# A second level of product sums on GpSimd, eight transposes for sixteen, and routing as a sign, in a gated long-convolution and attention layer

## The reference, cut to what matters

```python
def _L0_xattn_ref(k, v, q, ssm_kernel, D, head_dim):     # k = v = ctx, q = layernorm(x)
    kv = einsum('bhil,bhjl->bijhl', k_, v_)              # products of every two rows of a group
    y = causal convolution of kv with ssm_kernel (by FFT)
    out = y + kv * D
    out = einsum('bijhl,bhil->bjhl', out, q_)            # weighted by q, summed over i (8 terms)

def _L0_ffn_ref(x, conv_w, Wq, Wk, Wv, Wg, router_w, Wout):   # 16 heads, DK 256, DV 512
    x = silu(x_prev * conv_w[:, 0] + x * conv_w[:, 1])
    q, k, v, g = silu(x @ Wq), x @ Wk, x @ Wv, x @ Wg
    q, k = rotary(q), rotary(k)
    logits = einsum('bhld,hdr->bhlr', v, router_w)       # RATIO = 2 routes
    scores = softmax(logits); onehot = one_hot(argmax(scores), 2)
    norm = 1 / running count of onehot
    q_exp = q[..., None, :] * (scores * onehot)[..., None] * norm
    k_exp = k[..., None, :] * onehot[..., None]
    qk = (q_exp @ k_exp^T) * HDK ** -0.5, lower triangle
    o = layernorm over each head of (qk @ v)
    return (silu(g) * o) @ Wout

x = x + tanh(g_xattn) * _L0_xattn_ref(ctx, ctx, layernorm(x), ...)
x = x + tanh(g_ffn) * _L0_ffn_ref(layernorm(x), ...)
```

## Time and profile before

| what | value |
|---|---|
| median of 3 executions | 910.64 us (909.43 to 911.76) |
| the profiled execution | 909.48 us, its span 907.7 us |
| PE busy | 863.7 us, 95% of the span |
| DVE busy | 712.7 us, 79% |
| POOL busy | 725.8 us, 80% |
| ACT busy | 434.6 us, 48% |
| chain that ended last | 88% of it on PE |

### The profile page before, as it was taken

How to read it: one execution, slowest core, us unless ns; L and a number is a source line. 1 busy time by engine, 2 the same in 40 slices (tenths; PEclk the granted TensorE clock), 3 DMA queues, 4 the chain that set the end, 5 groups by cost and what they waited for, 6 DMA issues and landing times.

```text
span 907.7 us, 17997 instructions
## 1 busy us (share of the span) xinstructions
PE 863.7 (95%) x6592; PEld 732.3 (81%) x6592; DVE 712.7 (79%) x1521; ACT 434.6 (48%) x941; POOL 725.8 (80%) x611
## 2 busy tenths in 40 slices
PE   4889999999999999999999999999999999999974
PEld 3768888888888888888888888888888888888762
DVE  4788877787887778788777878877787897778741
ACT  3655455444545544454554544455454545544320
POOL 6779888899888889988888998888899888886331
PEclk9999999999999999999999999999999999999995
DMA  9310222211222221122222112222211222210000
GB/s 268 106 53 1 65 65 65 64 32 36 63 65 65 65 64 35 34 63 66 64 65 65 38 30 63 65 65 65 65 40 28 63 65 65 65 48 12 4 15 18
DMA packets 26679, 51.83 MB, mean 57 GB/s; under 512 B 3232, under 2 KB 4640, under 8 KB 26592
## 3 DMA queue, kind: packets, MB, share of 16 engines
q1 hardware_dynamic: 22320, 46.19, 19.1%
q10 hardware_dynamic: 4272, 4.48, 1.5%
HBM read 42.12 MB, written 8.55 MB: 56 GB/s over the span
## 4 chain that ended last, share of the span: by engine, by line
PE 88%; issue 4%; DVE 3%; POOL 2%; ACT 1%; DMA 1%; POOLq 0%; SPq 0%; ACTq 0%; DVEq 0%
PE bank L335 38%; PE bank L306 24%; PE bank L284 9%; PE bank L293 6%; PE bank L387 4%; PE bank L372 4%; PE bank L319 2%; PE bank L322 1%; DVE z_terms L844 1%; DMA z_terms<-in_L_xattn_D 1%; PE bank L445 0%; POOL kv L695 0%; POOL rstd L710 0%; POOLq L67 0%; POOL o_rstd L710 0%
## 5 line engine op out<-in xcount | busy, mean ns | idle before, releaser
L306 PE MATMUL bank<-kv_pair,toep 128*128 128x512 f32 x960 | 244.9, 401 | 1.3 <-DVE z_terms L835 1.3
L704 POOL TENSOR_TENSOR kv_pair<-kv,kv_pair 128x576 fp32r<-128x576 f32 x126 | 179.0, 1432 | 51.3 <-ACT kv_pair L537 51.3
L306 PEld LDWEIGHTS bank<-kv_pair,toep 128*128 128x128 f32 x960 | 175.0, 189 | 41.7 <-DVE z_terms L835 6.7
L695 POOL TENSOR_TENSOR kv<-kx 128x512 f32<-128x512 f32 x128 | 173.0, 1351 | 5.6 <-DMA kx<-in_ctx 3.9
L710 POOL TENSOR_TENSOR o_rstd<-o_ve,minus_half 128x16 f32<-128x16 f32 x32 | 93.1, 2908 | 83.5 <-DVE o_ve L921 83.5
L537 ACT ACTIVATE kv_pair<-kv 128x576 fp32r<-128x576 f32 x128 | 87.8, 687 | 106.8 <-POOL kv L698 105.9
L335 PE MATMUL bank<-w_all_high,yT_high 128*128 128x512 f32 (+2 forms) x512 | 120.9, 358 | 0.8 <-DVE gated L952 0.8
L844 DVE TENSOR_TENSOR z_terms<-z_terms 128x512 f32<-128x512 f32 (+1 forms) x96 | 116.6, 1240 | 0.0
L335 PE MATMUL bank<-w_all_low,yT_high 128*128 128x512 f32 (+2 forms) x512 | 112.6, 342 | 0.0
L1017 DVE SCALAR_TENSOR_TENSOR out_sb<-bank,gates,x 128x512 f32<-128x512 f32 x32 | 24.0, 751 | 106.0 <-PE bank L335 106.0
L335 PE MATMUL bank<-w_all_high,yT_low 128*128 128x512 f32 (+2 forms) x512 | 105.9, 339 | 0.0
(11 more groups left out here) (110 smaller groups left out, 1595.9 us busy)
## 6 DMA issues: line engine op xcount, KB each, us to landing
toep<-taps_dram SPq DMA_DIRECT2D x31, 512.0 KB, 7.1
kx<-in_ctx SPq DMA_DIRECT2D x32, 384.0 KB, 7.4
x_in<-in_x SPq DMA_DIRECT2D x32, 256.0 KB
out_x<-out_sb SPq DMA_DIRECT2D x32, 256.0 KB
wv_t<-in_L_ffn_Wv ACTq DMA_DIRECT2D x1, 1024.0 KB, 8.0
w_g<-in_L_ffn_Wg ACTq DMA_DIRECT2D x1, 1024.0 KB, 6.9
w_out<-in_L_ffn_Wout ACTq DMA_DIRECT2D x1, 1024.0 KB, 10.5
w_qk<-in_L_ffn_Wq ACTq DMA_DIRECT2D x1, 512.0 KB, 4.5
```

The costliest lines, as they stand in the source:

```text
L306: ins = nc.tensor.matmul(bank[lc % 2][:, :], toep[:, 1 - p, a, (lc - mc) * P:(lc - mc + 1) * P], kv_p[b][:, 1 - p, mc, 0:FULL], start=(mc ...
L695: eng.tensor_tensor(view(kv[:, c % 2, 0:FULL], [[ROW, NROT], [1, ROW]]), view(kx[:, p, c, 0:ROW], [[0, NROT], [1, ROW]]), view(kx[:, p, c, ...
L704: eng.tensor_tensor(kv_p[1][:, p, c, :], kv[:, c % 2, :], kv_p[0][:, p, c, :].bitcast(F32), ALU.subtract).then_inc(kv_ready[c], 1)
```

## The change

- `add_halves` now runs twice in a step: chunks 0 and 1, and chunks 2 and 3 together. A second level of sums, `add_quarters`, runs on POOL, in two instructions in each step (chunks 0 and 1, then 2 and 3; each adds 2 x 256 columns to 2 x 256 columns). They stand in POOL's list after the rotary sum and ahead of products 2 and 3 (in step -1 after them). `add_transposed` transposes two blocks for each chunk, 8 matmuls instead of 16, and waits for `quarter_done` of POOL instead of `sum_done` of DVE.
- PE projects the gate ahead of `add_transposed`.
- The two `sel` comparisons go; `u` is made twice as wide in one instruction. POOL's rotary sum writes straight into `qke`, and its two products with the sine become one. DVE's `signed_copy` writes a second copy of q and k, times +1 or -1, in place of `expand`. Scores of two rows with different signs cancel, those with equal signs count twice, and the mask's scale is halved. `signed_copy` stands ahead of `ratio` and `gatedT_low` in DVE's list, right behind the second `add_halves`.
- DVE multiplies o by the gate first (`o_gated`, before `norm_x`), and by the power later. The projection of v waits for `o_gated`.
- ACT's gate and its round of products 2 and 3 change places with each other and with the copies of `qke`.

```diff
@@ tensor
-                    eng.wait_ge(sum_done[max(c, 1)], h1 + 1)
-                    for i in range(NROT):
+                    eng.wait_ge(quarter_done[c // 2], h1 + 1)
+                    for i in range(NROT // 2):
...
-                        eng.wait_ge(o_normed, h)
+                        eng.wait_ge(o_gated, h)
                     project(bank[4], yT_p, w_all_p, V0, DV, v_ps, y_low, h + 1)
...
+                if back:
+                    if can_wait(h):
+                        eng.wait_ge(mask_done[2], h)
+                    if h == 0:
+                        eng.wait_ge(g_low, 1)
+                    project(bank[5], yT_p, w_all_p, G0, DV, g_ps, y_low, h + 1)
                 if front:
                     if pre and h != -1:
                         eng.wait_ge(qx_ready, h + 3)
                     add_transposed(h + 1)
@@ scalar
+                if back:
+                    eng.wait_ge(g_ps, h + 1)
...
+                    eng.activation(gate_sb[:, :], bank[5][:, :], ACT.Silu).then_inc(gate_ready, 1)
                 if pre and h != -1:
                     kv_round(p, 2, h + 2)
-                    kv_round(p, 3, h + 2)
...
+                if pre and h != -1:
+                    kv_round(p, 3, h + 2)
@@ gpsimd
+            def add_quarters(half, h1):
+                eng.wait_ge(sum_done[2 * half + 1], h1 + 1)
+                n = NROT // 2 * ROW
+                z = z_terms[:, 2 * half:2 * half + 2, :]
+                eng.tensor_tensor(z[:, :, 0:n], z[:, :, 0:n], z[:, :, n:2 * n], ALU.add).then_inc(quarter_done[half], 1)
...
-                    for a in range(2):
-                        s = const[:, C_SIN + a * hf:C_SIN + a * hf + 1]
-                        eng.tensor_tensor(rot_b[:, :, a * hf:(a + 1) * hf], qk_sb[:, :, (1 - a) * hf:(2 - a) * hf],
-                                          view(s, [[0, 2 * RH], [1, hf]]), ALU.mult).then_inc(rot_prod, 1)
-                    eng.wait_ge(rot_prod, 3 * h + 3)
-                    eng.tensor_tensor(rot_a[:, :, :], rot_a[:, :, :], rot_b[:, :, :], ALU.add).then_inc(rot_ready, 1)
+                    sin = const[:, C_SIN:C_SIN + 1]
+                    eng.tensor_tensor(view(rot_b[:, 0, 0:1], [[HDK, 2 * RH], [hf, 2], [1, hf]]),
+                                      view(qk_sb[:, 0, hf:hf + 1], [[HDK, 2 * RH], [-hf, 2], [1, hf]]),
+                                      view(sin, [[0, 2 * RH], [hf, 2], [1, hf]]), ALU.mult).then_inc(rot_prod, 1)
...
+                    eng.tensor_tensor(qke[:, :, :, 0], rot_a[:, :, :], rot_b[:, :, :], ALU.add).then_inc(rot_ready, 1)
+                if front and h != -1:
+                    add_quarters(0, h + 1)
+                    add_quarters(1, h + 1)
                 if pre:
                     products(t, p, 2, h + 2)
                     products(t, p, 3, h + 2)
+                if h == -1:
+                    add_quarters(0, h + 1)
+                    add_quarters(1, h + 1)
@@ vector
-            def expand():
...
+            def signed_copy():
+                eng.scalar_tensor_tensor(out=qke[:, :, :, 1], in0=qke[:, :, :, 0], scalar=2.0,
+                                         in1=view(u[:, 0, 0:1], [[1, 2 * RH], [0, HDK]]), op0=ALU.mult, op1=ALU.mult
+                                         ).then_inc(qke_ready, 1)
...
+                    eng.wait_ge(gate_ready, h)
...
+                    eng.tensor_tensor(gated[:, :], bank[4][:, :], gate_sb[:, :], ALU.mult).then_inc(o_gated, 1)
                 if pre and h != -1:
                     norm_x(t, p, h)
...
-                    d = view(bank[6][:, DK:DK + 1], [[0, 2], [1, RH]])
-                    eng.tensor_scalar(sel[:, :, :, 0], d, 0.0, None, ALU.is_le)
-                    eng.tensor_scalar(sel[:, :, :, 1], d, 0.0, None, ALU.is_gt)
-                    eng.tensor_scalar(u[:, :], bank[6][:, DK:DK + RH], 0.0, 0.5, ALU.is_gt, ALU.subtract).then_inc(u_ready, 1)
+                    eng.tensor_scalar(u[:, :, :], view(bank[6][:, DK:DK + 1], [[0, 2], [1, RH]]), 0.0, 0.5, ALU.is_gt, ALU.subtract).then_inc(u_ready, 1)
...
                     eng.tensor_tensor(gated[:, :].rearrange("p (a n) -> p a n", n=HDV),
-                                      bank[4][:, :].rearrange("p (a n) -> p a n", n=HDV),
-                                      view(o_rstd[:, 0:1], [[1, RH], [0, HDV]]), ALU.mult).then_inc(o_normed, 1)
...
+                                      gated[:, :].rearrange("p (a n) -> p a n", n=HDV),
+                                      view(o_rstd[:, 0:1], [[1, RH], [0, HDV]]), ALU.mult).then_inc(gated_ready, 1)
...
                     multiply(p, 3, h + 1)
-                    add_halves(slice(2, 3), h + 1)
-                    add_halves(slice(3, 4), h + 1)
+                    add_halves(slice(2, 4), h + 1)
...
+                    eng.wait_ge(u_ready, h + 1)
+                    signed_copy()
```

More of the change, by code:

```diff
@@ L116, in flamingo_gated_layer @@
         ad = sb("ad", RH)
-        u = sb("u", RH)
-        sel = sb("sel", 2, RH, RATIO)
+        u = sb("u", 2, RH)
         th = sb("th", RH)
@@ L208, in flamingo_gated_layer @@
         sum_done = [sem(f"sum_done{i}") for i in range(CH)]
+        quarter_done = [sem(f"quarter_done{i}") for i in range(2)]
         (mul_last, y_conv, out_ready, ad_ready, u_ready, th1_ready, rth1_ready, ratio_ready, eps_ready,
          qke_ready, bn1_done, mv1_done, ve1_ready, nmr1_ready, qn_ready, x2_ready, bn2_done, mv2_done,
-         ve2_ready, nmr2_ready, z_ready, o_summed, o_ve_ready, o_normed, gated_ready) = (
+         ve2_ready, nmr2_ready, z_ready, o_summed, o_ve_ready, o_gated, gated_ready) = (
             sem(n) for n in ("mul_last", "y_conv", "out_ready", "ad_ready", "u_ready", "th1_ready", "rth1_ready",
@@ L214, in flamingo_gated_layer @@
                              "nmr1_ready", "qn_ready", "x2_ready", "bn2_done", "mv2_done", "ve2_ready",
-                             "nmr2_ready", "z_ready", "o_summed", "o_ve_ready", "o_normed", "gated_ready"))
+                             "nmr2_ready", "z_ready", "o_summed", "o_ve_ready", "o_gated", "gated_ready"))
         FIRST, LAST = -2, NH
@@ L444, in step @@
                     eng.wait_ge(qk_copied, h + 1)
-                    nc.tensor.matmul(bank[6][:, 0:RH], rank, u[:, :], start=True, stop=True).then_inc(cnt_ps, 1)
+                    nc.tensor.matmul(bank[6][:, 0:RH], rank, u[:, 0, :], start=True, stop=True).then_inc(cnt_ps, 1)
                 if pre and h != -1:
@@ L949, in step @@
                     eng.wait_ge(o_rstd_ready, h)
-                    if can_wait(h - 1):
-                        eng.wait_ge(gatedT_ps, h - 1)
+                    eng.wait_ge(o_gated, h)
                     eng.tensor_tensor(gated[:, :].rearrange("p (a n) -> p a n", n=HDV),
-                                      bank[4][:, :].rearrange("p (a n) -> p a n", n=HDV),
-                                      view(o_rstd[:, 0:1], [[1, RH], [0, HDV]]), ALU.mult).then_inc(o_normed, 1)
-                    eng.wait_ge(o_normed, h)
-                    eng.wait_ge(gate_ready, h)
-                    eng.tensor_tensor(gated[:, :], gated[:, :], gate_sb[:, :], ALU.mult).then_inc(gated_ready, 1)
+                                      gated[:, :].rearrange("p (a n) -> p a n", n=HDV),
+                                      view(o_rstd[:, 0:1], [[1, RH], [0, HDV]]), ALU.mult).then_inc(gated_ready, 1)
                 if back:
@@ L974, in step @@
                                       gatedT_p[0][:, :, :].bitcast(F32), ALU.subtract).then_inc(gatedT_ready, 1)
-                if h == 0:
-                    eng.wait_ge(qk_low, 1)
-                    eng.wait_ge(g_low, 1)
-                if back:
-                    eng.wait_ge(rot_ready, h + 1)
-                    if can_wait(h):
-                        eng.wait_ge(keT_ps, h)
-                        eng.wait_ge(qeT_ps, h)
-                    expand()
                 if setup_step:
@@ L1039, in shape_constants @@
     centre = np.eye(P) - heads @ heads.T / HDV
-    parts = [np.eye(P), same * HDK ** -0.5, rank, cos, cos, -sin, sin, np.eye(P)[:, ::-1], centre, heads]
+    parts = [np.eye(P), same * HDK ** -0.5 / 2, rank, cos, cos, -sin, sin, np.eye(P)[:, ::-1], centre, heads]
     return np.concatenate([a.astype(np.float32) for a in parts], axis=1)
```

39 lines of the change are left out of this document (21 added, 18 removed).

## The result

The changed kernel takes 913.59 us (median of 7 executions, 910.84 to 915.5), the kernel before 910.32 us beside it (7 executions, 908.37 to 911.76). The ratio is 1.0041, with a 95% interval of 1.0024 to 1.0058: slower by 0.4%. That is a small loss, and the two ranges overlap, but the interval leaves out 1. The prediction was 916 us, 897 to 934.

What follows compares the result with a forecast made beforehand. TensorE (PE) was taken to bound each step. Profiled 909.48 us plus 29 full steps x 0.2 minus 1 at the edges gave 914.3; the median 1.16 above made 915.5, rounded to 916 us, range 897 to 934.

Steps and rivals of the forecast that it cites:

- The blocks: DVE instructions with two SBUF inputs and POOL products or sums exclude each other; held ones end 0.56 to 1.20 us later.
- the layout: DVE and POOL rows of a full step laid out by that exclusion; last quarter add ends at 458.06, +0.1 us a step.
- First close call: POOL's cosine, issued 0.03 us after the second product of `multiply_last`, might win; then net +0.3 us a step.
- the two other orders: Cosine ahead of that product, +0.3 us a step, or add of chunks 0 and 1 ahead of the cosine, +0.5.
- the queue: Ten DVE and POOL instructions from 448.6 on pass one at a time; their own times add up to 9.4 us.
- PE's side: In each full step eight fewer transposes save 0.88 us; the last four come 1.0 us late with refill.
- The edges: Steps outside the full ones: +1.5 us in step -1, savings in steps 30 to 32; together -1 us.
- the signs: Expected after the change: POOL quarter adds of 1.6 to 1.8 us, PE idle 0.7 to 1.2, steps of 26.5 to 27.0.
- The cover for z: In a full step z is ready about 0.4 us early, so PE transposes it without a wait.
- POOL's late finish is absorbed: POOL idles 1.63 us before o's power, so its delay isn't handed on to the next step.
- o times gate first: `o_gated` comes 4 us before `o_normed` did; the projection of v gains slack and no time.
- The rival in time: Second quarter add done by 457.0, so PE's saving is kept, down to 884 us; chance 0.23.

Runs made afterwards that it cites:

- e3: The changed kernel with DVE's signed copy moved behind `ratio` and `gatedT_low`; 908.52 us, 0.9984 of the kernel before.
- e7: The changed kernel with DVE multiplying o by the power first and the gate second again; 907.2 us, 0.997 of the kernel before.
- e5: The changed kernel with quarter adds on DVE in two instructions, POOL's products 2 and 3 held for them; 882.25 us, and 881.41 us beside e8.
- e8: The kernel before with only the sums' part of e5, without the sign or the new order of o's products; 889.6 us, ratio 0.9783.
- e6: The changed kernel with one more POOL product of 192 columns between the quarter adds; 932.0 us, 1.0242 of the kernel before.
- e2: The changed kernel with the gate's projection behind the transposes of the sums again; 1040.17 us, 1.1428 of the kernel before.

## Why the prediction was right

- **The blocks** were right. Moved by 6.86 us, the layout gave 456.96, 458.04, 459.19, 459.75 and 460.92 for cosine, first add, sine, product of o and rotary sum; the rows say 456.96, 458.04, 459.21, 459.76 and 460.92. It gave 464.92 for the last quarter add; it ended at 464.98.
- **First close call**: the cosine, issued 0.03 us behind the second product of `multiply_last`, lost (0.41 us for DVE, 1.54 for POOL). So the order of the main layout held, and neither of the two other orders came. The x power, from 454.90 to 455.45, didn't block `multiply_last` either (the product of 455.04 took its 0.42 us inside it), for which the prediction had 924 us. The Trainium skill, page SBUF — State Buffer (Who interferes with whom), has whoever issues first hold the shared pair of ports for the whole instruction, and the other blocked until then. These rows disagree: both ran at once, neither longer than alone (0.55 and 0.42 us).
- **A close call that I missed**: DVE's second add was laid out as issued at 453.98, 0.08 us ahead of POOL's quarter add. It waits 0.1 us for its own products' signal (460.93 to 461.03), so the quarter add went first. The sum of turns is nearly the same, the end moved by 0.06 us.
- **A miscount**: the prediction has ten instructions in the queue, 6 of POOL and 4 of DVE or so, with 9.4 us. Its own layout has five of POOL and four of DVE, 9.11 us; the other 0.35 us is the end of `multiply_last`. The layout and the sum don't use the count.
- **PE's side**: wait and refill 1.02 us against 1.0; net +0.16 us in this step. The main layout alone gave 0.1; the forecast took 0.2 for an order that didn't come. Between the transposes of steps 1 and 30 the kernel before takes 767.0 us and the changed one 771.0: +4.0 where the sum had 5.8.
- **The edges were wrong in size and in sign**, +1.6 for -1. At the transposes of step 1 the changed kernel is 4.4 us behind and not 1.5. In step -1 x2 comes 2.2 us later: two adds of 1.28 were laid out, but the first, issued at 28.72, waits for DVE's second add, and the two take 3.48 us. Around step 0 PE waits 1.65, 1.66 and 2.43 us in a row, the last for z, whose transposes open step 1 at 68.62 for 66.73: 1.9 us behind. The other 2.5 us come right after, where the granted clock is 0.50 for some 6 us. The kernel before has it at 1.00 there and at 0.50 earlier, for some 3 us from 59.1 on. The term had no row for the clock. The tail gave 2.8 us back; I had 2.2.

Two stretches of the changed kernel at the turn from step 0 to step 1 (busy time of PE, PEld, DVE, ACT and POOL, then the granted clock, the DMA share and GB/s):

```profile
68.00:71.00 3.00, 2.38 (x8) 2.09 (x9) 1.44 (x3) 1.71 (x5) 3.00 (x3) 0.50 0.37 144
71.00:74.00 3.00, 3.00 (x19) 1.93 (x21) 2.54 (x7) 0.68 (x1) 3.00 (x5) 0.50 0.00 0
```

Here PE is busy for all of the second stretch and still at half the clock. Sum of the spans: 4.4 + 4.0 - 2.8 = 5.6, as 913.3 - 907.7. The medians differ by 3.3 us; executions of the changed kernel spread over 4.7 us, and the profiled one is among the longer ones, 1.6 us above its median, where the prediction set the median 1.16 us above the profiled execution.

- **Part of the number is luck.** The steps were put 1.8 us too high and the edges 2.6 us too low, and the two nearly cancel: 914.3 us for the profiled execution, 915.21 measured. The range of 897 to 934 holds the kernel before as well, so the number tests little; the lengths and the order of the rows carry the mechanism. Of the signs, one was half right: only the second quarter add was long (1.65 us), the first took 1.31.
- **The cover for z** held in the full steps but the first: PE waits for z only at the start of step 1, the 2.43 us above. "POOL's late finish is absorbed" held by little: e3 shows it handed on once the step is 0.2 us shorter.
- **o times gate first** was priced as slack and no time. Its 0.6 us was in the layout, but not as a cost that could be saved; e7 shows some 6 us (9.0 us less between the transposes of steps 1 and 30, 2.7 us more at the edges).
- **The rival in time** was right about the prize (884 us): e5 reaches 882 us, though by another way than that rival's, with the quarter adds on DVE and POOL's products held.

## What to carry to other kernels

Before work goes from a full TensorE to GpSimd, list the VectorE instructions with two SBUF inputs and the GpSimd ones between the last free point and the moment when the result is due, and add their free durations: they pass one at a time, and the total decides, not either engine's busy share. Here the quarter adds on VectorE, with GpSimd's own work held back by one wait, gave 3.1% together with the other edits and 2.2% alone (e5, e8), where on GpSimd they gave -0.4%. An early instruction with slack, put ahead of such a queue, isn't free: 0.6 us of it cost 0.2 to 0.4 us at the end of the queue (e7).

## What the runs showed of the hardware

- TensorE kept 2.4 GHz through waits of 0.86 us (the changed kernel) and 1.38 us (e6) in each step, and was granted 1.2 GHz after two waits of 1.40 and 2.09 us with four transposes between them (e2), for some 3 us. That was a third of e2's loss. In step 0 of the kernel before it was granted 1.2 GHz after waits of 1.11, 0.76 and 0.96 us with transposes between them, each shorter than e6's 1.38.
- A DVE product with two SBUF inputs runs undisturbed beside a 2.91 us GpSimd power of 16 values (0.42 us), but a GpSimd power of one value that starts behind such a product is delayed by it (0.71 us for 0.55). A long DVE instruction holds that power up nearly to its own end: in step -1 of the kernel before, one of 2048 columns ends at 35.36, and the power ends 0.40 us after it.

```profile
33.24 2.52 POOL L710 TENSOR_TENSOR rstd<-ve,minus_half 128x1 f32<-128x1 f32 x1 [3.91 <-DVE ve L1001]
33.08 2.28 DVE L800 TENSOR_TENSOR w_all_low<-w_qk,w_all_high 128x2048 fp32r<-128x2048 f32 x1
```

- A GpSimd sum that writes every second element takes no longer: the rotary sum into `qke` took 1.63 us, as its contiguous form did (1.61). Both of these lengths include a wait for DVE; the shortest over all steps is 1.28 us for each form.
